# Decoder layer on one core: query norms one step earlier and on ScalarE, two transposes moved to VectorE, loads reordered, and the values' delay cut from 20 to 18 steps

## What is computed

```python
q = _causal_conv_silu(x @ Wq, qcw, qcb).reshape(b, t, HK, DK)      # 16 heads of 128
k = _causal_conv_silu(x @ Wk, kcw, kcb).reshape(b, t, HK, DK)
v = _causal_conv_silu(x @ Wv, vcw, vcb).reshape(b, t, HK, VE)      # 256 values a head
q, k = _l2norm(q), _l2norm(k)
alpha, beta = sigmoid(x @ Wa), sigmoid(x @ Wb)
def step(state, inp):                                              # over the 64 tokens
    state = state * at
    err = vt - einsum('bhkv,bhk->bhv', state, kt)
    state = state + bt * einsum('bhk,bhv->bhkv', kt, err)
    ot = einsum('bhkv,bhk->bhv', state, qt)
out = outs.reshape(b, t, HV * DV) @ Wo
```

## Time and profile before

| what | us |
|---|---|
| median of 3 runs (2484.18 to 2489.06) | 2485.99 |
| the profiled execution, its own time | 2486.33 |
| its span, first to last instruction | 2484.7 |
| TensorE busy over the span | 2146.1 (86%) |
| VectorE, ScalarE, GpSimd busy | 1858.5, 1473.8, 1090.4 |

### The profile page before, as it was taken

The page is one execution under the profiler, slowest core; times in us unless marked ns, Lnnn a source line. Parts: engine busy times, 40 slices in busy tenths (PEclk is TensorE's granted clock), DMA queues, the critical chain, the costliest instruction groups (busy, mean ns, idle before and its releaser), DMA issues.

```text
span 2484.7 us, 66235 instructions
## 1 busy us (share of the span) xinstructions
PE 2146.1 (86%) x23576; PEld 1370.0 (55%) x23576; DVE 1858.5 (75%) x2925; ACT 1473.8 (59%) x2755; POOL 1090.4 (44%) x1440
## 2 busy tenths in 40 slices
PE   2376769989998898999899899999988888999998
PEld 2133335555555565555555555555555567777776
DVE  7675667978887787888779788888856556776665
ACT  3475646666666666666566666666656535555554
POOL 1015574654737366373736638374571012222222
PEclk9898989999999999999999999999989999999999
DMA  7546543233333324333332433333242110111100
GB/s 289 160 106 135 124 93 83 85 84 93 85 83 92 84 76 89 87 85 83 91 85 76 91 89 82 90 94 85 69 90 61 37 55 12 32 40 41 33 20 18
DMA packets 507447, 205.37 MB, mean 83 GB/s; under 512 B 437584, under 2 KB 462928, under 8 KB 505168
## 3 DMA queue, kind: packets, MB, share of 16 engines
q1 hardware_dynamic: 507088, 200.76, 32.0%
HBM read 128.33 MB, written 72.35 MB: 81 GB/s over the span
## 4 chain that ended last, share of the span: by engine, by line
PE 51%; DVE 12%; issue 12%; SPq 10%; ACT 8%; DMA 5%; POOL 1%; ACTq 0%; DVEq 0%; POOLq 0%
PE PS L1278 15%; PE PS L1292 9%; DVE Y L1028 6%; PE PS L1516 3%; PE PS L1356 3%; PE PS L1445 3%; PE PS L1478 3%; PE PS L1372 2%; PE PS L1329 2%; SPq L377 2%; PE PS L1506 2%; ACT XN L796 2%; DMA SCR<-PGD 2%; PE PS L1464 2%; SPq L431 2%
## 5 line engine op out<-in xcount | busy, mean ns | idle before, releaser
L1028 DVE SCALAR_TENSOR_TENSOR Y<-PS,CW,Y 128x504 f32<-128x504 f32 (+2 forms) x1536 | 1115.4, 732 | 404.5 <-ACT Y L770 350.7
L770 ACT ACTIVATE Y<-PS,CW 128x512 f32<-128x512 f32 x512 | 398.5, 778 | 395.1 <-PE PS L1278 384.6
L1292 PE MATMUL PS<-WOS,XN 128*128 128x256 f16 x3072 | 389.7, 278 | 4.3 <-DVE XN L1043 3.3
L1292 PEld LDWEIGHTS PS<-WOS,XN 128*128 128x128 f16 x3072 | 307.0, 100 | 108.1 <-issue 12.1
L1278 PE MATMUL PS<-XV,WH 128*128 128x512 f16 x1024 | 322.2, 398 | 32.3 <-DMA XV<-XHD 20.1
L1278 PE MATMUL PS<-XK,WH 128*128 128x512 f16 x1024 | 312.5, 387 | 16.3 <-DMA XK<-XHD 16.2
L632 POOL TENSOR_TENSOR SQ<-KQ 128x512 f32<-128x512 f32 x128 | 138.1, 1079 | 427.5 <-PE PS L1320 335.7
L618 POOL TENSOR_TENSOR SCR<-SCR 128x31 f32<-128x31 f32 (+15 forms) x496 | 282.1, 569 | 38.9
L615 POOL TENSOR_TENSOR SCR<-SCR 128x31 f32<-128x31 f32 (+15 forms) x496 | 268.7, 542 | 33.0
L796 ACT ACTIVATE XN<-PS,KN 128x256 f32<-128x256 f32 x512 | 212.6, 466 | 71.7 <-PE PS L1292 71.7
L1043 DVE TENSOR_TENSOR XN<-Y,XN 128x512 f16<-128x512 f32 x256 | 202.8, 792 | 12.5 <-ACT Y L777 12.5
(11 more groups left out here) (141 smaller groups left out, 3124.9 us busy)
## 6 DMA issues: line engine op xcount, KB each, us to landing
PGD<-SCR SPq DMA_DIRECT2D x128, 256.0 KB, 2.2
SCR<-PGD SPq DMA_DIRECT2D x128, 256.0 KB, 3.0
EQD<-XN SPq DMA_DIRECT2D x32, 512.0 KB, 4.1
SCR<-EQD SPq DMA_DIRECT2D x128, 128.0 KB, 2.8
SCR<-QND SPq DMA_DIRECT2D x128, 128.0 KB, 3.2
SCR<-in_wall SPq DMA_DIRECT2D x8, 1024.0 KB, 5.9
SCR<-PGD SPq DMA_DIRECT2D x64, 128.0 KB, 3.3
ED<-SCR SPq DMA_DIRECT2D x16, 512.0 KB, 2.7
```

Source lines behind the costliest of these rows:

```text
L770: A_.activation(Y[:, b, :], PJ[b][:, :], ACT.Identity, scale=CW[:, h[1] % NH, cw0 + 3:cw0 + 4], bias=CW[:, h[1] % NH, cw0 + 4:cw0 + 5]).th ...
L1028: V_.scalar_tensor_tensor(yv[:, :, m:T], pv[:, :, 0:T - m], CW[:, h[1] % NH, cw0 + 3 - m:cw0 + 4 - m], yv[:, :, m:T], ALU.mult, ALU.add).t ...
L1292: ins = mm(VWB[:, E * i:E * i + E], VHL[:, vk, n, P * a:P * a + P], WOS[:, wk, 2 * (w[1] % NH) + n, :], start=(t == 0), stop=(t == 5))
```

## The change

It has six parts.

- **Squares and query sums.** The squares are taken by ScalarE (an ACTIVATE with Square), right behind the silu of the queries, and query_sums is done for head k-1 in step k instead of for head k-2. In full steps it stays at its place on TensorE. In the build-up it moves behind project 2, and ahead of decays and grams. The grams now wait for this same head's copy of the sums (`qs_ev` of k-1).
- **Transposes.** Beta is transposed on VectorE once, in 32 x 32 blocks, before it is stored, so that a batch's beta comes with one transfer of 128-byte rows. The key norms are transposed on VectorE once a batch (`lane_scales`) straight into KN; their way through DRAM (KND) is gone.
- **Loads.** `load_values` becomes `load_pair` (EN and T1, now issued two heads ahead) and `load_gram` (PGV, one head ahead as before). XK's first load goes to the head part. `load_lanes` moves from behind the spill to the front of its step, `store_lanes` from step 8 of a batch to step 7, its completion is awaited at the front of the next step.
- **GpSimd** starts a batch one step earlier and has no work per step.
- **Written-out loop.** `eng.Fori` becomes a Python loop: every step has its own instructions.
- **AHEAD** is 2 instead of 4, so v = k - 18, and `AT_STEP` packs the 28 units into 17 steps instead of 18.

```diff
-AHEAD = 4
+AHEAD = 2
-        AT_STEP = [1] * 8 + [2] * 10 + [0, 0]
+        AT_STEP = [1] * 6 + [2] * 11 + [0]
-            with eng.Fori(0, LOOPS) as g:
+            for g in range(LOOPS):
                 for h in range(2, NH + 2):
                     step((g, h), (g, h + NH + AHEAD))
...
+                if g == 3:
+                    sp.wait_ge(S["st_xh0"], at(16))
+                    sp.dma_start(XK[:, :, :], XHD[0]).then_inc(S["ld_xk"], 16)
...
-            sp.wait_ge(S["gate_v"], at(4))
-            sp.dma_start(BED, BEA.rearrange("p g h a -> p (g h a)")).then_inc(S["st_be"], 16)
+            sp.wait_ge(S["gate_v"], at(6))
+            sp.dma_start(BED, BET).then_inc(S["st_be"], 16)
...
             def load_beta(k):
                 g, off = k
                 if after(k, 8):
-                    sp.wait_ge(S["lane"], batches(k, LANE_OPS))
+                    sp.wait_ge(S["lane"], batches(back(k, 8), LANE_OPS, 7))
                     sp.nop(nofuse=True)
-                for q in range(4):
-                    src = BED[32 * q:32 * q + 32].rearrange("i (b l) -> b i l", l=BL)[ds(g * 2 + off // 8, 1)]
-                    sp.dma_start(BLN[32 * q:32 * q + 32, :], src.rearrange("o i l -> (o l) i"),
-                                 allow_slow_non_contiguous=True).then_inc(S["ld_bl"], 16)
+                src = BED.rearrange("p (b i) -> b p i", i=BL)[ds(g * 2 + off // 8, 1)]
+                sp.dma_start(BLN[:, :], src.rearrange("o p i -> (o p) i")).then_inc(S["ld_bl"], 16)
...
             def step(v, k):
                 ph = k[1] % 8
-                if ph == 1 and exists(back(k, 17)):
-                    sp.wait_ge(S["st_le"], batches(back(k, 17), 48, 48))
+                if v is not None and ph == 0 and exists(back(k, 16)):
+                    sp.wait_ge(S["st_le"], batches(back(k, 16), 32, 32))
                     sp.nop(nofuse=True)
+                if ph == 1 and exists(back(k, 8)) and not (v is None and k[1] > NH):
+                    load_lanes(back(k, 8))
...
                 if v is None and k[1] == NH + AHEAD - 1:
-                    stored_eq(UNITS)
-                    load_values((0, 0))
+                    store_lanes((0, 0))
+                    sp.wait_ge(S["st_le"], at(32))
+                    load_pair((0, 0))
+                    load_gram((0, 0))
+                    load_lanes((0, 8))
                 if exists(v):
-                    v1 = (v[0], v[1] + 1)
+                    v1, v2 = (v[0], v[1] + 1), (v[0], v[1] + 2)
+                    if exists(v2) and v2[1] % 2 == 0:
+                        load_pair(v2)
                     if exists(v1):
-                        load_values(v1)
+                        load_gram(v1)
...
-                if ph == 1 and exists(back(k, 8)):
-                    load_lanes(back(k, 8))
...
-                if exists(back(k, 2)):
-                    spill_q(back(k, 2))
-                if ph == 0 and exists(back(k, 16)):
-                    store_lanes(back(k, 16))
+                if exists(back(k)):
+                    spill_q(back(k))
+                if v is not None and ph == 7 and exists(back(k, 15)):
+                    store_lanes(back(k, 15))
...
-            def squares(k):
-                pool.wait_ge(S["silu2"], heads(k, 1, 1))
-                pool.wait_ge(S["qs_mm"], heads(k))
-                nc.gpsimd.tensor_tensor(SQ[:, :], KQ[:, k[1] % 2, 1, :], KQ[:, k[1] % 2, 1, :], ALU.mult).then_inc(S["sq"], 1)
...
+            def squares(k):
+                act.wait_ge(S["silu2"], heads(k, 1, 1))
+                act.wait_ge(S["qs_mm"], heads(k))
+                A_.activation(SQ[:, :], KQ[:, k[1] % 2, 1, :], ACT.Square).then_inc(S["sq"], 1)
...
+            V_.transpose(BET, BEA.rearrange("p g h a -> p (g h a)")).then_inc(S["gate_v"], 1)
...
+            def lane_scales(k):
+                dve.wait_ge(S["lane"], batches(k, LANE_OPS, 5))
+                if after(k, 16):
+                    dve.wait_ge(S["vw_ev"], heads(back(k, 8), 2))
+                dve.nop(nofuse=True)
+                V_.transpose(KN[:, (k[1] // 8) % 2, :], KNL[:, :]).then_inc(S["kn_done"], 1)
...
+                if k[1] % 8 == 6 and exists(back(k, 14)):
+                    lane_scales(back(k, 14))
```

More of the change, by code:

```diff
@@ new lines, in load_pair @@
+                u = (off // 2) % 2
+                l0 = 4 * (off % 8)
+                if after(w, 4):
+                    sp.wait_ge(S["nu_mm"], heads(back(w, 2)))
+                    sp.nop(nofuse=True)
+                for q in range(4):
+                    sp.dma_start(EN[u][32 * q:32 * q + 32, :, (q % 2) * 32:(q % 2) * 32 + 32],
+                                 ED[b, 32 * q + l0:32 * q + l0 + 8, :].rearrange("o l (j i) -> (o j) l i", j=BL)).then_inc(S[f"ld_en{u}"], 16)
+                if after(w, 4):
+                    sp.wait_ge(S["m_done"], heads(back(w, 2)))
+                    sp.nop(nofuse=True)
@@ L385, in load_values, with load_gram @@
+                for n in range(2):
+                    src = QND[b].rearrange("o p i -> (o p i)").rearrange("(l n t) -> n l t", n=2, t=T)[n, l0:l0 + 8, :]
+                    sp.dma_start(T1[u][64 * n:64 * n + 64, :, :], src[None, :, :].broadcast_to([T, 8, T])).then_inc(S[f"ld_t{u}"], 16)
+            def load_gram(w):
+                g, off = w
+                s = off % 2
                 if after(w, 2):
@@ L387, in load_values @@
                     sp.nop(nofuse=True)
[L388 removed]
+                sp.dma_start(PGVF[s], PGD[ds(g * 2 + off // 8, 1), :, off % 8, :].rearrange("o p x -> (o p) x")).then_inc(S[f"ld_pv{s}"], 16)
             def spill(k):
@@ L590, in lanes_begin @@
                 pool.wait_ge(S["ld_lp"], batches(k, 64, 64))
-                pool.wait_ge(S["ld_bl"], batches(k, 64, 64))
+                pool.wait_ge(S["ld_bl"], batches(k, 16, 16))
+                if after(k, 8):
+                    pool.wait_ge(S["kn_done"], batches(k))
                 pool.nop(nofuse=True)
@@ L636, in step @@
                 if exists(kb):
-                    if ph == 2:
+                    if ph == 1:
                         lanes_begin(kb)
-                    if ph >= 2:
-                        for j in range(JCUT[ph - 2], JCUT[ph - 1]):
+                    if 1 <= ph <= 6:
+                        for j in range(JCUT[ph - 1], JCUT[ph]):
                             lanes_row(kb, j)
-                    if ph == 7:
+                    if ph == 6:
                         lanes_end(kb)
-                if exists(back(k, 1)):
-                    squares(back(k, 1))
             schedule(pool, step)
@@ L791, in values @@
                 act.wait_ge(S["out_mm"], heads(w))
-                act.wait_ge(S[f"ld_kn{kn}"], groups(w, 64, 64))
+                act.wait_ge(S["kn_done"], batches(w, 1, 1))
                 for i in range(2):
@@ L812, in step @@
             def step(v, k):
-                w, kp, kq = (None if v is None else back(v)), back(k), back(k, 2)
+                w, kp = (None if v is None else back(v)), back(k)
                 if begins(v):
@@ L819, in step @@
                     silu_kq(kp, 2)
+                    squares(kp)
                 if exists(v):
@@ L1335, in correction @@
                 pe.wait_ge(S["n_ev"], heads(v, 1, 1))
-                if exists(back(k, 2)):
-                    pe.wait_ge(S["qs_ev"], heads(back(k, 2), 1, 1))
+                if exists(back(k)):
+                    pe.wait_ge(S["qs_ev"], heads(back(k), 1, 1))
                 pe.nop(nofuse=True)
@@ L1363, in grams @@
                     pe.wait_ge(S["m_done"], heads(v, 1, 1))
-                if exists(back(k, 2)):
-                    pe.wait_ge(S["qs_ev"], heads(back(k, 2), 1, 1))
+                pe.wait_ge(S["qs_ev"], heads(kp, 1, 1))
                 for b in (2, 3):
@@ L1386, in step @@
                     off_diagonal(v)
-                if exists(back(k, 2)):
-                    query_sums(back(k, 2))
+                if exists(back(k)) and v is not None:
+                    query_sums(back(k))
                 if exists(v):
@@ L1397, in step @@
                     project(k, 2, XK, "ld_xk")
+                if exists(back(k)) and v is None:
+                    query_sums(back(k))
                 for n in units[:1]:
```

53 lines of the change are left out of this document (14 added, 39 removed).

## The result

The changed kernel takes 2358.0 us, the median of four runs (2356.3 to 2362.0), against 2485.1 us: a ratio of 0.948, 95% interval 0.946 to 0.951. The forecast was 2338, the range 2304 to 2380. The profiled execution took 2356.5 us with a span of 2354.8.

The account below looks back on a forecast made before the run. TensorE's own work, 12.15 of 12.30 us, was taken to bound a full step. Savings of 106 us in full steps and 42 in the build-up, 148 together, took 2486.3 to 2338 us; range 2304 to 2380.

Parts of the forecast that it names:

- Full steps: The 110 steps after the build-up: stalls and half-clock work go, saving 106 us, bounds 96 to 115.
- XV: XV's load at a group's end: of 19.8 us of waits, half a us stays at each of 7 ends, 3.5 us.
- PGV: PGV's load ahead of off_diagonal in full steps: all 38.3 us of waits go, with 0.6 us to spare.
- the rival's rule: Full steps: descriptors are consumed in order, so XV stays late behind the lanes' load; 2361 us at worst, chance 15%.
- Loop: The loop's jump back in full steps: written out, 12.2 us of TensorE waits go.
- Squares: Full steps: GpSimd's 10.6 us of waits go; the square on ScalarE costs nothing, with 0.95 us of cover.
- Build-up: From 103.4 to 342.9 us, before the full steps: 42 us saved, between 28 (full price) and 62 (no price).
- XK's preload: Start of the build-up: 10.7 us of waiting for XK's first load go, less 0.7 for beta's transpose: 10 us saved.
- the new wait: Build-up: sums wait for this step's square, delaying decays and grams; 1.7 us per two-unit step, 0.3 for others, +20 us.
- PGV's wait: Rival in full steps: a late store keeps PGV's 38.3 us of waits and 13.6 of clock; 2390 us, chance 10%.
- the loop's end: Rival: the "issue" gap is not the jump, so writing the loop out does nothing there; 2354 us, chance 3%.
- The slower case: Rival: written-out instructions arrive late, TensorE waits in each of 96 former loop steps; 2572 us at 2.4 us each, chance 4%.

## Why the prediction was right, and where not

**Full steps (106, measured 114.0).** The bound of 12.15 us of TensorE's work a step was right (12.29 in most steps), and so was the working: the stalls and the half clock behind them are one sum and go together. 83.3 us of idle time went, 77.4 forecast (80.9 less 3.5 for XV), and 30.8 us of busy time, 28.8 forecast. The terms:

- PGV: "all 38.3 us go, with 0.6 us to spare": 2.8 remain. The working was right in each step: project 0 starts at 489.14 there, the store is issued 2.9 us later (3 forecast) and PGV 11.3 (11.3). But what the forecast named as the reason, transfers that no longer stand ahead, is only part of it: with the four beta transfers back PGV has no more waits than without them, and with the short beta but the store a step later the waits are back.
- XV: half a us at each of 7 ends was too much; there is one wait, in the tail. The margin is small: the three edits that put XV later (beta, EN and T1, the store) each made TensorE wait for it. By the rival's rule, that of the Trainium skill ("DMA: Bandwidth & Descriptors", Queues, rings and completion order), XV would queue behind the lanes' short pieces. No run shows that it costs XV time: XV lands 4.2 us after its issue (median), though the last of the lanes' load lands only 1.1 to 1.5 us after that issue; before the change it was 4.4, and 4.5 in the run with EN and T1 one head ahead, where the lanes had landed before.
- Loop: the five turns were 12.2 us in the sum and 10.6 in the run that puts them back. But writing the loop out is worth 28: 10.6 for the turns, 8.7 for waits for PGV and XK that come back with SyncE's slower issuing, most of the rest half clock. The sum had that gain under PGV, and saw no link between the two.
- Squares: 10.6 us and their clock, measured alone 14.2. Costed at nothing in a full step: right, with 0.91 us of cover.

**Build-up (42, measured 18.0).** XK's preload brought 8.9 us at VectorE's first multiply of grams (119.0 instead of 127.9 us), 10 forecast. Four terms were wrong or missing:

- The step that failed is the size of the new wait: "I take 1.7 for 11 two-unit steps, and 0.3 for the others: +20". It measured 26 to 28. The place of the wait and its reason were right, and 1.7 is what a two-unit step at full clock pays (11.21 us against 9.4 to 9.9 with the sums later, 1.3 to 1.8). But every other two-unit step pays half clock besides (12.86 us, 3.1 to 3.5 more), for which the term had nothing. And one-unit steps pay 2.2 us, not 0.3, since their decays stand in the same circle.
- The square was costed at nothing, and checked only in the full step. In the build-up it lies on ScalarE's chain: 0.4 to 0.5 us in 17 steps, 8 us.
- The first PGV's wait, 8.7 us, was not seen. The order of SyncE showed it: the batch's store, the wait for it, EN, T1 and PGV all stand in the last step of the build-up. The forecast gave such waits 2 us, so 6.7 are missing.
- XK's second load, which the forecast left out, cost 8.5 instead of 5.5 us.

42 - 6 - 8 - 6.7 - 3 is 18 us, as measured. So close a fit is partly luck: the terms come from single edits, and two of these together kept 37.4 of 43.2 us.

**Rivals.** PGV's wait did not stay, XV was not late in the full steps, the loop's end went, and written-out steps were in time: 12.29 us. The slower case charged only written-out code with being brought in, but the profile's instruction queues moved 3.13 and 0.81 MB with the code written out, and 3.29 and 1.20 MB with the loop back. The far bound of the build-up, 28 us, was too good; a bound "at full price" has to charge the one-unit steps and the half clock as well. Two slips in the prediction's sums change nothing (3.2 + 3.28 + 0.7 is 7.2, not 7.3; 96 times 2.4 is 230, not 234).

## What to carry to other kernels

When an operation moves, check its cover in every stage that runs it: the square was free behind 0.91 us of room in a full step, and cost 0.4 to 0.5 of its 0.63 us in the build-up, where its engine is part of a circle of waits. In such a circle a delay does not fade; count everything queued between the late result and the instruction that feeds the next turn, and move independent work ahead of the wait. Where one engine issues all loads, several small savings on it (a store earlier, fewer issues, straight code) hold up one margin together: undoing one of three of them cost 15 to 29 us in the 110 steps here, and two at once 63.

## What the runs showed of the hardware

- TensorE in the two-unit steps of the build-up alternates between its two clocks. After the same 2.6 us of idling the decays take 1.02 us for two products in one step (granted clock 1.00, 2.4 GHz) and 1.91 in the next (0.50, 1.2 GHz), which makes steps of 11.21 and 12.86 us by turns. With the idle time at 0.4 us the long steps are gone but for two.
- SyncE issues the same four transfers over 1.99 us in straight code and over 2.81 us in the hardware loop. The loop brings in no less code: 4.49 MB of instructions were moved with it, 3.94 without.
- A part that no edit touched, the attention and feed-forward part, took 500.1 us in one execution and 510.9 in another, at a clock of 0.99 and 0.97. Runs of one kernel spread over 3 us in one group of runs and over 20 in another.
